# A GRU kernel on one core: W_hh and a stretch of x loaded in transfers of 126, 117, 120, 110 and fewer rows

## The reference

```python
x = x + conv(x, cond_2048[:, None, :])          # 16 taps, one filter a channel
def cell(h, x):
    gi = x @ W_ih + b_ih
    gh = h @ W_hh + b_hh
    r = sigmoid(i_r + h_r); z = sigmoid(i_z + h_z)
    n = tanh(i_n + r * h_n)
    return (1.0 - z) * n + z * h
x = x + scan(cell, cond_2048, x)                # 256 steps, one after the other
```

## Time and profile before

| | us |
|---|---|
| median of 3 runs | 978.94 (978.8 to 979.1) |
| the profiled execution | 979.08 |
| its span | 977.4 |
| TensorE busy in the span | 967.8 (99%) |
| VectorE busy | 877.7 (90%) |
| ScalarE, GpSimd busy | 544.2, 614.3 |
| granted clock of TensorE | full in every slice |

### The profile page before, as it was taken

One profiled execution on the slowest core, in us unless ns is written; L12 is line 12 of the kernel. 1 busy time (PEld: TensorE's weight loads), 2 busy tenths in 40 slices (PEclk: granted clock), 3 DMA queues, 4 the chain that ended last, 5 costly groups with the idle time before them and its releaser, 6 DMA issues.

```text
span 977.4 us, 65406 instructions
## 1 busy us (share of the span) xinstructions
PE 967.8 (99%) x27158; PEld 792.0 (81%) x27158; DVE 877.7 (90%) x3075; ACT 544.2 (56%) x2309; POOL 614.3 (63%) x1790
## 2 busy tenths in 40 slices
PE   9999999999999999999999999999999999999997
PEld 6788888888888888888888888888888888888775
DVE  7789999999999999999999999999999988887565
ACT  4334455655555655655655555555556555556543
POOL 7556666666666666666666666666666666666642
PEclk9999999999999999999999999999999999999999
DMA  8731001010010101101010010100101010000000
GB/s 305 72 46 41 20 16 42 12 38 20 20 41 12 38 16 32 31 17 38 12 36 25 21 37 14 36 20 25 36 17 32 12 31 20 15 25 5 26 15 13
DMA packets 67608, 32.54 MB, mean 33 GB/s; under 512 B 44528, under 2 KB 65648, under 8 KB 67312
## 3 DMA queue, kind: packets, MB, share of 16 engines
q1 hardware_dynamic: 66880, 28.25, 11.3%
q10 hardware_dynamic: 432, 0.11, 0.0%
HBM read 19.86 MB, written 8.49 MB: 29 GB/s over the span
## 4 chain that ended last, share of the span: by engine, by line
PE 92%; POOL 3%; issue 3%; DVE 2%; ACT 0%; POOLq 0%; DVEq 0%
PE pg L993 64%; PE pg L758 8%; PE pcv L768 5%; PE pg L768 4%; PE pcv L788 3%; PE pcv L778 3%; PE pg L778 3%; POOL wt L495 1%; PE pg L788 1%; POOL nzh L723 1%; PE pg L748 1%; PE pcv L1016 1%; DVE x L1226 0%; DVE hp L1314 0%; PE pcv L758 0%
## 5 line engine op out<-in xcount | busy, mean ns | idle before, releaser
L993 PE MATMUL pg<-whh,hp 128*32 128x192 f32 x16384 | 714.9, 326 | 4.3 <-DVE hp L1314 3.1
L993 PEld LDWEIGHTS pg<-whh,hp 128*32 128x32 f32 x16384 | 519.6, 110 | 136.1 <-DVE hp L1314 14.9
L1244 DVE SCALAR_TENSOR_TENSOR pcv<-xb,cnd,pcv 128x256 f32<-128x256 f32 (+2 forms) x588 | 315.3, 536 | 6.9
L1196 ACT ACTIVATE rz<-gt 128x64 f32<-128x64 f32 x512 | 136.5, 267 | 271.3 <-DVE gt L1289 246.5
L723 POOL TENSOR_TENSOR nzh<-rz,hp 128x32 f32<-128x32 f32 x512 | 157.4, 307 | 171.6 <-ACT rz L1196 170.1
L1289 DVE STREAM_TRANSPOSE gt<-pg 128x128 f32<-128x128 f32 x512 | 161.4, 315 | 47.4 <-PE pg L993 40.4
L1201 ACT ACTIVATE nzh<-an 128x32 f32<-128x32 f32 x512 | 121.4, 237 | 130.2 <-DVE an L1301 130.2
L1314 DVE TENSOR_TENSOR_SCAN hp<-zcp,nzh 128x96 f32<-128x96 f32 x512 | 174.3, 340 | 12.3 <-ACT nzh L1201 9.7
L1301 DVE TENSOR_TENSOR_SCAN an<-rz,gn 128x64 f32<-128x64 f32 x512 | 152.7, 298 | 26.0 <-ACT rz L1196 26.0
L1198 ACT ACTIVATE zcp<-gt 128x32 f32<-128x32 f32 x512 | 111.0, 217 | 0.0
L1293 DVE STREAM_TRANSPOSE gn<-pg 128x64 f32<-128x64 f32 x512 | 106.9, 209 | 0.0
(11 more groups left out here) (147 smaller groups left out, 1081.7 us busy)
## 6 DMA issues: line engine op xcount, KB each, us to landing
xb<-x SPq DMA_DIRECT2D x96, 94.0 KB, 2.1
out<-x SPq DMA_DIRECT2D x60, 128.0 KB, 1.8
wih<-w_ih SPq DMA_DIRECT2D x4, 768.0 KB, 8.0
whh<-w_hh SPq DMA_DIRECT2D x4, 512.0 KB, 12.2
windows<-x SPq DMA_DIRECT2D x24, 64.0 KB, 3.4
whh<-w_hh SPq DMA_DIRECT2D x4, 256.0 KB, 13.8
xb<-x SPq DMA_DIRECT2D x16, 62.0 KB, 2.4
tz<-taps SPq DMA_DIRECT2D x12, 64.0 KB, 3.3
```

Source lines behind the costliest of these rows:

```text
L993: i = pe.matmul(gates(t // 2, f)[D * j:D * (j + 1), 0:IN], hp[:, t % 2, 2 * c + 1 - t % 2:2 * c + 3 - t % 2, :, 1].rearrange("p u b -> p ( ...
L1196: act.activation(rz[:, f, :, :, 1].rearrange("p g (c b) -> p (g c) b", b=B), gt[:, f, :, u], ACT.Sigmoid).then_inc(s_rz[f], 1)
L1244: dve.scalar_tensor_tensor(x1_of(c, a, b)[:, lo:hi] if lag == K - 1 else sums, xx[:, c, (K - 1 - lag) * B + lo:(K - 1 - lag) * B + hi], cn ...
```

## The change

The transfers of W_hh are given lists of row ranges: the r and z columns of the last chunk in 120 and 8 rows, the n columns of chunks 1, 2 and 3 in 126 and 2, 117 and 11, 110 and 18 rows. The second stretch of x goes in 112, 6, 4, 3, 2 and 1 rows and is issued ahead of SyncE's wait for chunk 2, so right behind W_hh. The wait stays, behind it. The waits for W_hh and for x count the larger number of transfers.

```diff
+        ROWS_RZ = [[(0, P)], [(0, P)], [(0, P)], [(0, 120), (120, P)]]
+        ROWS_N = [[(0, P)], [(0, 126), (126, P)], [(0, 117), (117, P)], [(0, 110), (110, P)]]
+        ROWS_X = [(0, 112), (112, 118), (118, 122), (122, 125), (125, 127), (127, P)]
...
             for c in range(C):
-                sp.dma_start(whh[:, c, F:], w_hh[:, c, 0:2 * F]).then_inc(s_whh[c], 16)
-                sp.dma_start(whh[:, c, 0:F], w_hh[:, c, 2 * F:]).then_inc(s_whh[c], 16)
-            sp.wait_ge(s_whh[C - 2], 32)
-            sp.dma_start(xb[1][:, 0, :], x[:, 0, B:(W2 + TB) * B]).then_inc(s_xe, 16)
+                for a, b in ROWS_RZ[c]:
+                    sp.dma_start(whh[a:b, c, F:], w_hh[a:b, c, 0:2 * F]).then_inc(s_whh[c], 16)
+                for a, b in ROWS_N[c]:
+                    sp.dma_start(whh[a:b, c, 0:F], w_hh[a:b, c, 2 * F:]).then_inc(s_whh[c], 16)
+            for a, b in ROWS_X:
+                sp.dma_start(xb[1][a:b, 0, :], x[a:b, 0, B:(W2 + TB) * B]).then_inc(s_xe, 16)
+            sp.wait_ge(s_whh[C - 2], 16 * (len(ROWS_RZ[C - 2]) + len(ROWS_N[C - 2])))
...
-                pe.wait_ge(s_whh[c], 32)
+                pe.wait_ge(s_whh[c], 16 * (len(ROWS_RZ[c]) + len(ROWS_N[c])))
...
-                    dve.wait_ge(s_xe, 16)
+                    dve.wait_ge(s_xe, 16 * len(ROWS_X))
```

## The result

| | before | after |
|---|---|---|
| median of 5 runs, us | 978.91 (978.8 to 979.1) | 982.29 (981.67 to 983.82) |
| ratio, 95% interval | | 1.0036 [1.0025, 1.0047] |
| the profiled execution, its span | 979.08, 977.4 | 983.82, 982.1 |

The change makes the kernel 3.4 us slower, 0.36%. The profiled execution of after is the slowest of its five, 4.7 above the one of before; a sum made from the two traces is to be held against 4.7, not 3.4.

What follows compares the result with a forecast made beforehand. Late W_hh transfers were taken to delay the recurrence's start, ceiling 1.34 us. A gain of 0.9 less 0.1 for extra transfers gave 979.08 - 0.8 = 978.28 profiled, less 0.14 a median of 978.14 (likeliest 978.1); range 977.4 to 979.6.

Steps and rivals of the forecast that it cites:

- one engine is late before the change: W_hh loads before the first step: one late DMA engine holds back chunks 1 to 3, stalling TensorE 1.34 us.
- the extra issues are hidden: SyncE's queue: W_hh goes from 8 to 12 issues, x from 1 to 6, about 0.5 us each, nothing on the path.
- x's place is worth nothing: Second stretch of x behind the weights: lands near 23, not 24.3, its reader is at 29.61; no gain.
- the dealing: DMA transfers: equal shares to as many of 16 engines as the rows divide into, always from the first engine on.
- Rival 4: W_hh loads: odd row counts dealt to very few engines, chunk 2 or 3 8 us late, 987 us; chance 3%.
- one engine takes 0.08 us for 2 KB: Price of moved W_hh load at 410 GB/s: last engine gains 3.2 us, the one before it 1.9.
- first engines lose 0.80 us: W_hh remainders on the first DMA engines: 10 more units of 2 KB on the first two, costing 0.80 us.
- Being behind on every engine's queue it doesn't delay c3: x queued behind W_hh takes 0.9 us after the weights and doesn't delay the last chunk.
- The choice that I called the weakest: W_hh loads: the late engine is among those spared, giving 977.6 to 978.5 us; chance 63%.
- Rival 3: W_hh loads: the late engine is among the loaded ones, up to 0.80 us more, 979.3 to 979.7 us; chance 20%.
- The range: Whole kernel's time: 977.4 to 979.6 us, likeliest 978.1; 13% left outside.
- no gain: W_hh row split: the same engines serve the remainders, so nothing comes of it, 978.7 to 979.2 us; chance 12%.

Runs made afterwards that it cites:

- cut by columns: Kernel before, W_hh in as many transfers as in the change but split by columns, 128 rows each, x as before: 979.16 us, ratio 1.0001.
- the halves: Kernel before with the change's four cut W_hh transfers split into rows 0 to 63 and 64 to 127, x as before: 981.16 us, ratio 1.0021.
- two queues: Same four W_hh transfers split in rows 0 to 63 and 64 to 127, the second parts issued by ScalarE on its own queue: 982.64 us, ratio 1.0038.

## Why the prediction was wrong

**What held.** That one engine is late before the change (c2's last two landings come at 20.32 and 20.99 us, the other 30 by 19.54); that every us lost or won before the first step is found again at the end (4.73 in the start, 4.7 in the span); that nothing else on the path waits for what moved (taps, windows, SyncE's wait); that the extra issues are hidden (cut by columns: 0.11 us); that x's place is worth nothing (978.96 against 979.05); the dealing, also as the rule quoted there gives it. The sums of the prediction come out as written. Rival 4, odd counts dealt to one engine, is out.

**The step that failed** is the price: "one engine takes 0.08 us for 2 KB", taken from 397 to 424 GB/s of transfers of 128 rows and used for 126, 120, 117 and 110 rows. The rate isn't a property of the engines alone. With the change it fell to 156 to 338 GB/s at a share near 1. The term "first engines lose 0.80 us" should have stood beside a far larger one for all of them: of the 2.70 us that W_hh alone costs, 120 rows alone bring 1.72, 110 rows 0.64 and 126 rows 0.31. These three sum to 2.67 and leave nothing for the 117 rows, so the single figures are shares only roughly; the cuts overlap in time. The Trainium skill, "SBUF - State Buffer", section "Door 1: The DMA port swizzle", says that partitions share sixteen ports by a fixed pattern, and that 0 to 63 reach only eight of them and 64 to 127 the other eight. Its factor of two for 64 rows agrees with the packets out of SBUF (468 ns against 236); into SBUF they took 1.5 to 1.6 times as long (344 and 380 ns against 234). By the same pattern partitions 32 apart share a port. If 120 rows go to the engines in consecutive blocks of 8, engines whose blocks lie 32 rows apart meet at the same ports, which would fit the 416 ns; but no run here shows the ports or which rows an engine has.

**The second step that failed**: "Being behind on every engine's queue it doesn't delay c3". Behind on each engine's queue isn't behind on the others'. x in one piece of 128 rows did no harm, in six pieces 0.76 us; with the cut of c3 alone, c2 came 1.8 us later, through its last two landings. So much is shown. That engines which are through go on to the pieces behind and crowd the late engine at its place in SBUF is argued from it.

**The choice that I called the weakest**, 63% for a late engine among the last ones, has nothing for it in the runs, as far as the slower packets let one see: with 126 rows, which spare the last two, c1 began no earlier (19.23), and with 110 rows, which spare the last five, c3 moved away from c2 (2.36 us). Rival 3 was nearer in sign, but its mechanism (0.8 us of load) is not what cost 3.4 us: the halves, with no load moved, cost 2.13.

**The range** should have had a bound for packets that take twice as long. The cut transfers hold 1280 KB; at half of 410 GB/s they would take 3.2 us more, 982.1 without any gain, near the measured 982.29. That it is so near is partly luck: the cut of W_hh alone cost 2.70, x brought the rest, and uncut transfers slowed too. "Don't bother", the rule for two transfers to disjoint halves in the Trainium skill, "DMA: Bandwidth & Descriptors", section "Rules for kernel authors", was read as "no gain"; measured, cutting four transfers in halves costs 2.13 us.

**Open.** Why two queues brought the halves no relief, where I had forecast it, and why the last landing of c3 came 1.4 us later there. That engines which pick packets of either half independently meet by chance as often as in step would fit, but no run tests it. Why 126 rows slow uncut transfers in the kernel and not themselves alone. Which engine is late, what 117 rows cost in place, and what the remainders of 2, 8, 11 and 18 rows cost by themselves weren't tried either.

No version tried beats the kernel before. x early in one piece is the same within the interval.

## What to carry to other kernels

Price a transfer by its rows as well as by its bytes, and by what is in flight beside it: load SBUF with all 128 partitions, and cut by columns if it has to be cut. A share of the DMA engines near 1 tells only that they are occupied; read the GB/s beside it (1.00 went with 188 here). A transfer queued behind can slow the one ahead, as c3's cut slowed c2.

## What the runs showed of the hardware

Alone, 64 rows of 6 KB into SBUF take 4.25 us and 128 rows 4.14; from HBM to HBM 3.35 and 4.69. 120 rows of 6 KB into SBUF take 5.69 us, 1.55 more than 128. The median packet of 6 KB takes 234 ns in HBM for any of the row counts tried, and into SBUF 234 with 128, 126 and 117 rows, 276 with 110, 303 with 112, 344 and 380 with 64 and 416 with 120. A transfer of 120 rows is served by 15 engines, of 117 by 13. A cut of the last chunk of W_hh alone made the chunk ahead of it 1.8 us later. A cut of 126 and 2 rows slowed the 4 KB packets of uncut transfers from 159 to 209 ns.
